# Attention over field pairs: rows fetched one by one from SyncE and ScalarE, the first lookup's numbers spread by TensorE

## The reference

```python
emb = jax.vmap(lambda tbl, idx: tbl[idx], in_axes=(0, 1), out_axes=1)(embed_tables, sparse)   # 2048 x 26 x 32
bi = emb[:, FIRST, :] * emb[:, SECOND, :]                                                     # 2048 x 325 x 32
a = jax.nn.relu(jnp.einsum('bpd,dh->bph', bi, att_w_w) + att_w_b)                             # 8 hidden units
scores = jnp.einsum('bph,ho->bpo', a, att_d_w) + att_d_b
att_weight = jax.nn.softmax(scores, axis=1)
att_out = jnp.sum(att_weight * bi, axis=1)
out = jax.nn.sigmoid(jnp.concatenate([att_out, dense], axis=-1) @ fin_w + fin_b)
```

## Time and profile before

| | before |
|---|---|
| runs | 483.49, 484.43, 484.66 us |
| profiled execution, its own time | 483.39 us |
| its span, first to last instruction | 481.6 us |
| TensorE busy | 450.2 us (93%), 2280 matmuls |
| VectorE busy | 372.6 us (77%) |
| GpSimd busy | 347.9 us (72%), 372 instructions |
| ScalarE busy | 95.8 us (20%) |
| mean granted TensorE clock | 0.996 of full speed |

### The profile page before, as it was taken

One profiled execution on the slowest core, in us unless ns is written; L12 is line 12 of the kernel. 1 busy time (PEld: TensorE's weight loads), 2 busy tenths in 40 slices (PEclk: granted clock), 3 DMA queues, 4 the chain that ended last, 5 costly groups with the idle time before them and its releaser, 6 DMA issues.

```text
span 481.6 us, 6198 instructions
## 1 busy us (share of the span) xinstructions
PE 450.2 (93%) x2280; PEld 177.6 (37%) x2280; DVE 372.6 (77%) x645; ACT 95.8 (20%) x198; POOL 347.9 (72%) x372
## 2 busy tenths in 40 slices
PE   0699999999998999999999899999999899999884
PEld 0354443343333533333333443333334344333221
DVE  6337788796965979799775969879786788887985
ACT  0000101131252011112243101113234201114253
POOL 5777777777777777777777777777777777777740
PEclk9999999999999999999999999999999999999998
DMA  6933743121122223222112222213111222322210
GB/s 221 250 13 15 147 58 36 13 15 13 15 13 15 14 14 79 15 14 14 14 14 13 15 13 15 13 13 15 14 13 16 14 15 13 15 13 14 15 10 1
DMA packets 13661, 15.06 MB, mean 31 GB/s; under 512 B 6368, under 2 KB 12608, under 8 KB 13248
## 3 DMA queue, kind: packets, MB, share of 16 engines
q0 software_dynamic: 11776, 6.05, 23.1%
q1 hardware_dynamic: 1360, 7.53, 4.2%
q10 hardware_dynamic: 496, 1.09, 0.6%
HBM read 14.61 MB, written 0.03 MB: 30 GB/s over the span
## 4 chain that ended last, share of the span: by engine, by line
PE 78%; POOL 8%; DVE 5%; issue 4%; DMA 3%; ACT 1%; POOLq 0%; DVEq 0%
PE looked_own L391 33%; PE back_s L391 16%; PE first L405 13%; PE sums_f L415 12%; POOL emb L368 8%; PE sums_s L429 3%; DVE onehot L667 2%; DMA chunk_numbers<-index_chunk 1%; DMA emb<-tables,rows 1%; DMA chunk_of<-chunk_numbers 1%; PE back_f L442 1%; PE back_s L452 1%; DVE look_masked L678 1%; DMA par<-params 1%; DVE ring L691 0%
## 5 line engine op out<-in xcount | busy, mean ns | idle before, releaser
L368 POOL DMA_INDIRECT emb<-tables,rows x324 | 305.9, 944 | 98.7 <-issue 96.9
L691 DVE TENSOR_TENSOR ring<-emb_t,turned 128x512 f32<-128x512 f32 (+9 forms) x180 | 193.9, 1114 | 3.4
L391 PE MATMUL looked_own<-look_table,onehot 128*128 128x448 f32 x434 | 178.0, 554 | 17.0 <-DVE onehot L667 16.7
L391 PEld LDWEIGHTS looked_own<-look_table,onehot 128*128 128x128 f32 x434 | 79.5, 192 | 114.4 <-issue 114.4
L507 ACT ACTIVATE hidden<-first,par 128x512 f32<-128x512 f32 (+1 forms) x84 | 56.5, 678 | 284.7 <-PE first L405 284.4
L391 PE MATMUL back_s<-look_table,onehot 128*128 128x448 f32 x238 | 94.4, 545 | 3.1 <-DVE score L739 3.1
L405 PE MATMUL first<-ring,par 128*32 128x512 f32 (+1 forms) x672 | 90.7, 591 | 4.3 <-DVE ring L691 4.3
L415 PE MATMUL sums_f<-ring,par 128*32 128x512 f32 (+1 forms) x672 | 90.0, 583 | 0.0
L667 DVE TENSOR_TENSOR onehot<-chunk_of,turned 128x2048 f32<-128x2048 f32 (+1 forms) x24 | 48.3, 2018 | 26.6 <-PE looked_own L391 21.2
L391 PEld LDWEIGHTS back_s<-look_table,onehot 128*128 128x128 f32 x238 | 44.0, 190 | 51.7 <-issue 51.7
L368 POOL DMA_INDIRECT emb<-tables,rows_first x44 | 41.8, 950 | 17.2 <-issue 13.1
(11 more groups left out here) (56 smaller groups left out, 101.0 us busy)
## 6 DMA issues: line engine op xcount, KB each, us to landing
emb<-tables,rows POOLq DMA_INDIRECT x324, 3.2
look_table<-tables SPq DMA_DIRECT2D x3, 1568.0 KB, 8.2
chunk_of<-chunk_numbers SPq DMA_DIRECT2D x3, 768.0 KB, 4.9
chunk_of<-chunk_numbers ACTq DMA_DIRECT2D x1, 768.0 KB, 3.8
emb<-tables,rows_first POOLq DMA_INDIRECT x44, 3.8
par<-params ACTq DMA_DIRECT2D x1, 258.5 KB, 3.1
ids<-sparse SPq DMA_DIRECT2D x1, 208.0 KB, 2.5
feats<-dense SPq DMA_DIRECT2D x1, 104.0 KB, 8.1
```

Source lines behind the costliest of these rows:

```text
L368: pool.indirect_dma_start(emb[:, f, g * D:(g + 1) * D], None, stacked, bass.IndirectOffsetOnAxis(ap=row, axis=0),).then_inc(gathered[f], 16)
L391: mm = nc.tensor.matmul(looked_rows[look_bank[tile]], onehot[:, c, g * P:(g + 1) * P], look_table[:, n, c, :], start=c == 0, stop=c == CHU ...
L691: nc.vector.tensor_tensor(slot[:, at:at + n, :], emb_t[:, i:i + n, :], turned[:, f % 2, :].unsqueeze(1).broadcast_to((P, n, P)), ALU.mult) ...
```

## The change

1. **SyncE fetches seven tiles of field 24.** For tile 3 of quad 0 and tiles 2 and 3 of the quads 1 to 3, SyncE loads 32 row numbers at a time into registers and issues one DMA of 128 bytes for each row: 7 x 128 = 896 DMAs into a new buffer `emb_placed`. Tile 2 of quad 0 is gathered into that buffer by GpSimd, ahead of its field 13. ScalarE copies the placed columns into `emb` ahead of the groups of field 23 (`place_rows`).
2. **ScalarE fetches four tiles of field 23** (tile 3 of each quad) in the same way: 8 rows ahead of the groups of each of the fields 0 to 15, 128 DMAs per quad, 512 in all (`fetch_rows`), with 16 row numbers loaded at a time.
3. **GpSimd** loses these 11 tiles' gathers plus the placed one, gets the placed one back early and one gather for field 19 in the last quad: 368 - 12 + 1 + 1 = 358.
4. **TensorE** looks up 11 tiles instead of 12 in the last quad. Its last two steps, which stood beside the fields 15 and 16, are gone.
5. **The first lookup's numbers** no longer go through HBM: TensorE multiplies one column of the identity, broadcast, with `index_chunk` (four matmuls into PSUM, `chunk_first`), and VectorE compares from there, ahead of the second `make_rows`. Table 0 is loaded in two parts, and the first steps wait for the first part alone.
6. **Queues.** Table 1 follows table 0 at once; table 2 and the second quad's chunk numbers come after SyncE's first 32 rows, the third quad's behind its first three tiles and the last quad's behind its fifth. The dense features move to ScalarE's queue. VectorE computes the row numbers for 1 and 2 in six small operations.

The core of the diff:

```diff
+ROWS_SP = 32
+SP_FIELD = 24
+TILES_SP = (1, 2, 2, 2)
+PLACED = 2
+SP_PLACE = 23
+SP_FIRST = 13
+LAST_LOOK_TILES = (4, 4, 3)
+ROW_FIELD = 23
+ROWS_LOADED = 16
+ROWS_BESIDE = 8
+ROWS_BESIDE_FIELDS = range(16)
@@ block.sync
-            sp.wait_ge(transposed, 6)
-            load_table(2)
-            for q in range(2, QUADS):
-                load_chunks(q)
+            sp.wait_ge(sp_rows_ready, 1)
+            tiles = 0
+            for q in range(QUADS):
+                for i in range(PLACED - TILES_SP[q], PLACED):
+                    t = q * G + G - PLACED + i
+                    for p in range(0, P, ROWS_SP):
+                        if tiles == 0 and p == P // 4:
+                            load_table(2)
+                            sp.wait_ge(chunk_numbers_home, 16)
+                            load_chunks(1)
+                        _, at = nc.values_load_multi_w_load_instructions(
+                            sp_rows[t:t + 1, p:p + ROWS_SP], engines=(mybir.EngineType.SP,), min_val=0,
...
+                        for k in range(ROWS_SP):
+                            sp.dma_start(emb_placed[p + k:p + k + 1, q, i * D:(i + 1) * D],
+                                         stacked[bass.ds(at[k], 1), :]).then_inc(sp_gathered[tiles], 16)
+                    tiles += 1
+                if 0 < q < QUADS - 1:
+                    load_chunks(q + 1)
@@ block.tensor
+            pe.wait_ge(index_chunk_made, 1)
+            for g in range(G):
+                row = ident[0:QUADS * LOOKS * G, g:g + 1].broadcast_to((QUADS * LOOKS * G, P))
+                mm = nc.tensor.matmul(chunk_first[:, g * P:(g + 1) * P], row, index_chunk[:], start=True, stop=True)
+            mm.then_inc(chunk_first_spread, 1)
...
-                    pe.wait_ge(look_table_in[n], 16)
+                    pe.wait_ge(look_table_first_in if n == 0 and part == 0 else look_table_in[n], 16)
@@ block.scalar
+                def place_rows():
+                    act.wait_ge(placed_gathered, (QUADS * PLACED - sum(TILES_SP)) * 16)
+                    for i in range(sum(TILES_SP[:q]), sum(TILES_SP[:q + 1])):
+                        act.wait_ge(sp_gathered[i], P * 16)
+                    nc.scalar.activation(emb[:, SP_FIELD, PLACED_COLS], emb_placed[:, q, :], ACT.Copy
+                                         ).then_inc(placed, 1)
+                def fetch_rows(f):
+                    at = ROWS_BESIDE_FIELDS.index(f) * ROWS_BESIDE
+                    if at == 0 and q == 0:
+                        act.wait_ge(row_numbers_ready, 1)
+                    if at == 0 and q:
+                        act.wait_ge(transposed, (q - 1) * F + ROW_FIELD + 1)
+                    if at % ROWS_LOADED == 0:
+                        _, numbers[:] = nc.values_load_multi_w_load_instructions(
...
+                    for p in range(at, at + ROWS_BESIDE):
+                        act.dma_start(emb[p:p + 1, ROW_FIELD, (G - 1) * D:], stacked[bass.ds(numbers[p % ROWS_LOADED], 1), :]
+                                      ).then_inc(rows_fetched, 16)
+                fetch_rows(0)
                 for f in range(1, F):
+                    if f in ROWS_BESIDE_FIELDS:
+                        fetch_rows(f)
+                    if f == SP_PLACE:
+                        place_rows()
                     done = groups_of(f)
```

More of the change, by code:

```diff
@@ L58, in attention_fm, with look_tiles @@
     LOOKS = len(LOOK)
+    assert max(LAST_LOOK_TILES) <= G and LAST_LOOK_TILES[0] == LOOK_TILES[0]
     assert P * PART_ROWS >= V and P * PART_ROWS - V <= V and LOOK[-1] < F - 1 and CHUNK_ROWS * D <= PAIRS_C * P
-    steps = [(q, n, g, part) for q in range(QUADS) for n in range(LOOKS) for g in range(G - LOOK_TILES[n], G)
+    def look_tiles(q, n):
+        return LOOK_TILES[n] if q < QUADS - 1 else LAST_LOOK_TILES[n]
+    steps = [(q, n, g, part) for q in range(QUADS) for n in range(LOOKS) for g in range(G - look_tiles(q, n), G)
              for part in range(len(STEPS))]
@@ L68, in attention_fm, with tiles_through_look @@
     assert len(STEP_FIELDS) + END_STEPS == STEPS_Q and END_STEPS == len(STEPS)
-    def tiles_through_look(n):
-        return sum(LOOK_TILES[:n + 1])
+    def tiles_through_look(q, n):
+        return q * TILES_Q + sum(look_tiles(q, i) for i in range(n + 1))
     def first_step(q, n):
-        return q * STEPS_Q + (tiles_through_look(n) - LOOK_TILES[n]) * len(STEPS)
+        return (tiles_through_look(q, n) - look_tiles(q, n)) * len(STEPS)
     def steps_beside(q, f):
@@ L86, in onehots_for @@
     def onehots_for(numbers):
-        return [(steps[i][0], steps[i][1], steps[i][3]) for i in numbers if steps[i][2] == G - LOOK_TILES[steps[i][1]]]
+        return [(steps[i][0], steps[i][1], steps[i][3]) for i in numbers if steps[i][2] == G - look_tiles(*steps[i][:2])]
     def tiles_ended(numbers):
@@ L113, in taken_before, with gathers_of @@
         return max([t + 1 for t in range(tile) if look_bank[t] == look_bank[tile]], default=0)
-    def gathers_of(f):
+    def gathers_of(q, f):
         if f in LOOK:
-            return G - LOOK_TILES[LOOK.index(f)]
-        return G
+            return G - look_tiles(q, LOOK.index(f))
+        if f == ROW_FIELD:
+            return G - 1
+        return G - PLACED if f == SP_FIELD else G
+    assert ROW_FIELD not in LOOK and ROWS_BESIDE * len(ROWS_BESIDE_FIELDS) == P and ROWS_LOADED % ROWS_BESIDE == 0
+    assert ROWS_BESIDE_FIELDS[-1] < ROW_FIELD
+    PLACED_COLS = slice((G - PLACED) * D, G * D)
+    assert FIRST_FIELDS <= SP_FIRST < SP_PLACE < SP_FIELD and len(TILES_SP) == QUADS and max(TILES_SP) <= PLACED
+    assert SP_FIELD not in LOOK
     assert G * D == P and B % (P * G) == 0 and RING < GROUPS and 1 < END_GROUPS
@@ L211, in attention_fm @@
             "p (t f) -> p t f", f=F) for i in range(2))
+        row_clamped, row_wrap = (final[0:QUADS].rearrange("p g e -> p (g e)")[:, i * P:(i + 1) * P] for i in range(2))
+        index_clamped, index_wrap, index_part = (
+            final[0:QUADS * LOOKS * G].rearrange("p g e -> p (g e)")[:, G * P + i * P:G * P + (i + 1) * P] for i in range(3))
+        sp_clamped, sp_wrap = (weighed[0:T].rearrange("p g e -> p (g e)")[:, i * P:(i + 1) * P] for i in range(2))
         neg_max = sb("neg_max", [P, G])
@@ L251, in attention_fm @@
         rows_ready = sem("rows_ready")
+        sp_ids_in = sem("sp_ids_in")
+        sp_steps = sem("sp_steps")
+        sp_rows_ready = sem("sp_rows_ready")
+        sp_gathered = [sem(f"sp_gathered{i}") for i in range(sum(TILES_SP))]
+        placed_gathered = sem("placed_gathered")
+        placed = sem("placed")
+        row_ids_in = sem("row_ids_in")
+        row_steps = sem("row_steps")
+        row_numbers_ready = sem("row_numbers_ready")
+        rows_fetched = sem("rows_fetched")
         gathered = [sem(f"gathered{f}") for f in range(F)]
@@ L360, in _ @@
                         pool.wait_ge(rows_ready, 1)
-                    if q and gathers_of(f):
+                    if q == 0 and f == SP_FIRST:
+                        for n in range(QUADS):
+                            for i in range(PLACED - TILES_SP[n]):
+                                t = n * G + G - PLACED + i
+                                pool.indirect_dma_start(
+                                    emb_placed[:, n, i * D:(i + 1) * D], None, stacked,
+                                    bass.IndirectOffsetOnAxis(ap=rows[:, t, SP_FIELD:SP_FIELD + 1], axis=0),
+                                ).then_inc(placed_gathered, 16)
+                    if q and gathers_of(q, f):
                         pool.wait_ge(transposed, (q - 1) * F + f + 1)
-                    for g in range(gathers_of(f)):
+                    for g in range(gathers_of(q, f)):
                         if q == 0 and f < FIRST_FIELDS:
@@ L606, in _, with make_onehots @@
                                     ).then_inc(index_chunk_made, 1)
+            dve.wait_ge(par_in, 16)
+            dve.wait_ge(sp_ids_in, 16)
+            nc.vector.tensor_scalar(sp_clamped[:], sp_ids[:], float(-V), float(V - 1), ALU.max, ALU.min
+                                    ).then_inc(sp_steps, 1)
+            dve.wait_ge(sp_steps, 1)
+            nc.vector.tensor_scalar(sp_wrap[:], sp_clamped[:], 0.0, float(V), ALU.is_lt, ALU.mult).then_inc(sp_steps, 1)
+            dve.wait_ge(sp_steps, 2)
+            nc.vector.scalar_tensor_tensor(sp_rows[:], sp_clamped[:], float(SP_FIELD * V), sp_wrap[:], ALU.add, ALU.add
+                                           ).then_inc(sp_rows_ready, 1)
+            def make_onehots(of, n, part):
+                tiles, chunks = slice((G - look_tiles(of, n)) * P, G * P), STEPS[part]
+                numbers, here = chunk_of[:, of % 2, n, tiles], chunk_here
+                if of == 0 and n == 0:
+                    dve.wait_ge(chunk_first_spread, 1)
+                    numbers, here = chunk_first[:, tiles], par[:, cols["look_chunk"]]
+                else:
+                    dve.wait_ge(chunk_of_in[of % 2], (of // 2 + 1) * 16)
```

(17 more changed lines are left out.)

66 lines of the change are left out of this document (39 added, 27 removed).

## The result

| | before | after |
|---|---|---|
| runs beside each other | 484.55 us (483.49 to 484.75, 4 runs) | 489.95 us (489.01 to 491.27, 4 runs) |
| profiled execution, its own time | 483.39 us | 491.27 us |
| span | 481.6 us | 489.4 us |
| TensorE busy | 450.2 us, 2280 matmuls | 453.6 us, 2274 matmuls |
| mean granted clock | 0.996 | 0.984 |

The changed kernel is slower: ratio 1.0117, 95% interval 1.0092 to 1.0142. The forecast was 475.6 us and faster; the time came out as rival A's. The profiled execution is the longest of the four after, and the shortest of the four before, so the spans differ by 7.8 us where the medians differ by 5.4.

The account below looks back on a forecast made before the run. TensorE paces three quads; TensorE, VectorE's pair products and GpSimd's queue meet at the end. Gain 11.8 (start 6.4, tile 3.6, gather waits 1.8) less 3.0 for late relus, 8.8 us: 475.6 us, range 470 to 493.

Parts of the forecast that it names:

- rival A: ScalarE's rows, dearer than forecast, pace TensorE in the quads; gain gone at 0.456 us a row, 483 to 500 us; chance 0.20.
- I take 0.42: Price in us of each single-row DMA on SyncE and ScalarE, taken between bounds of 0.33 and 0.60.
- part 4: Cost of the single rows on SyncE and ScalarE: SyncE's hidden, ScalarE's late relus costing TensorE 3.0 us in all.
- break-even at 0.456: Row price in us on ScalarE at which late relus eat the whole gain of 11.8 us.
- rival B: Loading row numbers counts, so a SyncE row takes 0.60 us and SyncE sets the end, about 570 us; chance 0.07.
- 0.407 us a row is free; every 0.01 us above costs 0.96 us a quad: ScalarE in quad 1: row price allowed by 96 DMAs and four relus of 0.69 us ahead of TensorE's first score products.
- also hidden: SyncE's queue: table 2 and later quads' chunk numbers issue in time behind the rows, the last near 275 us, needed near 315.
- SyncE's rows hidden: SyncE's 896 rows at 0.42 us end at 383 us, in time for field 24 of the last quad; 0.49 allowed.
- Part 1, the start: First lookup at 10.0 us instead of 16.36, a gain of 6.4 us that goes through to the end if gathers are in time.
- Parts 2 and 3: Gathers stay in time, GpSimd 10 gathers or 12.5 us ahead at the end; the last quad's missing tile gains VectorE 3.6 us.
- part 3: End of the kernel: VectorE's path gains 6.4 + 3.6 + 1.8 = 11.8 us, GpSimd's 12.5; the later one, 11.8, counts.
- Rival C: Many small transfers delay gathers by 4 us through shared DMA engines, losing 4 to 8 us, 480 to 484 us; chance 0.10.

Follow-up runs that it names:

- the kernel with spread rows: Changed kernel with ScalarE's 512 rows placed 6 ahead of each of fields 0 to 11 and 8 ahead of 12 to 18; 485.85 us, ratio 1.0046 to the kernel before.
- the 474.64 us kernel: Changed kernel with ScalarE's rows spread over 19 fields and the last quad's chunk numbers issued right behind the third quad's; 474.64 us, ratio 0.9804 to the kernel before.
- the start alone: Kernel before with only the spread chunk numbers, split table and earlier table and chunk-number loads; no single rows, 368 gathers, 12 tiles; 484.56 us, ratio 1.0002.

## Why the prediction was wrong

**The step that failed: "I take 0.42" in part 4.** The issue alone was sized right, 0.42 us on SyncE and 0.38 on ScalarE. The loading of the numbers was named as an unknown and then priced at nothing: with it (1.30 us for 16 numbers, 0.08 a row) and the longer first row behind each load a row takes 0.481. The prediction's own line, wrong if a row costs over 0.45 us on ScalarE, was crossed. Rival A was the right mechanism, with 0.20: its formula at 0.481 gives 484.4 - 11.8 + 96 x 2.5 x 0.074 = 490.4, and 489.95 was measured. That it comes so near is in part luck, as the next paragraphs show; and where the formula has half a quad's loss in the last quad, the relus cost TensorE more there, 8.2 us of waits, than in either of the two before. The middle of the bounds, 0.33 and 0.60, is 0.465, also on the losing side; choosing low between them, with the break-even at 0.456, was a choice of the sign.

The Trainium skill, page "Runtime: NRT & Kernel Launch", section "Instruction fetch mechanics", gives about 200 ns a register for loads from HBM; here a number loaded from SBUF costs 0.081 us on ScalarE, and 2.15 us for 32, 0.067, on SyncE. By the page SyncE's row would have been 0.62, as the prediction worked out, and rival B right; the measurement decides, 0.48, and it lies between the page and the prediction's zero.

**"0.407 us a row is free; every 0.01 us above costs 0.96 us a quad": near, by two errors that cancel.** A relu hardly holds the issuing, though it runs 0.69 us:

```profile
177.56 0.23 ACTq L644 DMA_DIRECT2D emb<-tables  x1
177.84 0.69 ACT L588 ACTIVATE hidden<-first,par 128x512 f32<-128x512 f32 x1 [26.97 <-issue]
177.98 0.23 ACTq L644 DMA_DIRECT2D emb<-tables  x1
```

From one row to the next are 0.42 us with the relu between them, and 0.39 without ((196.72 - 193.98) / 7). So only the relu that TensorE waits for counts with its 0.69, the three ahead of it with 0.03 each, and the free price is about (41.8 - 0.8) / 96 = 0.427. TensorE's waits for relus in quad 1 come to 1.95 + 0.75 + 2.07 = 4.8 us rather than 96 x 0.074 = 7.1. But the waits also cost clock, which the prediction did not have. Behind the third of them TensorE's granted clock stood at the lower of its two levels for 3.4 us, 0.50 of full speed; with both stalls gone there is no such stretch in quad 1:

```profile
197.20:200.60 3.40, 2.79 (x16) 0.61 (x16) 0.23 (x1) 0.55 (x1) 2.48 (x4) 0.50 0.31 43
```

That is most of the 2.0 us more of busy TensorE. Together 6.8.

**Chunk numbers "also hidden": wrong, and covered.** At 0.479 a row the last quad's go out at 318.65, not 275, and the kernel with spread rows wants them 8.7 us before they land. Priced by experiment it is 485.85 to 474.64, 11.2 us. In the changed kernel itself they cost nothing, because the relus are later still. The step that failed is the same: the prediction had these numbers needed near 315, and issued at 275 at 0.42 us a row.

**SyncE's rows hidden: right, with nearly nothing to spare.** The budget was 0.49 us a row. In the 474.64 us kernel the last row goes out at 443.94, (443.94 - 8.55) / 896 = 0.486, and no wait for `emb_placed` shows. VectorE waits three times for ScalarE's copy of the placed columns, 2.8 us in all and never over 0.9; these waits are in the 474.64 us kernel too.

**Part 1, the start: nearly.** TensorE's lookups start at 10.29 (forecast 10.0). The first 14 take 8.48 us instead of 7.71, so the gain at their end is 5.3 us, not 6.4. They begin at half pace: the matmuls of 448 columns start 0.75 us apart until 16.3 us and 0.375 apart from there, before until 20.9, which is 6.0 us at half pace against 4.5. (The profile's records of the granted clock begin only at 16.3 and 20.8, so its 1.00 for the windows ahead of them says nothing.) With the same start the 474.64 us kernel had 3.6 us at half pace and took 7.26 for the 14, so this differs from run to run; what sets it no run here shows. The prediction took one length for granted.

**Parts 2 and 3.** 358 gathers, the last at 451.86 (forecast 450.7): right. The step from field 17 to 18 is 2.93 us (forecast 2.9): right, though the tile is worth 2.8 us in the end rather than 3.6, since VectorE then waits for gathers. Start and tile together: 484.2 - 474.6 = 9.6 us with the two stalls gone, where part 3 summed 11.8. So the gain that the prediction argued is there, less a fifth, and ScalarE's and SyncE's queues take all of it and more.

**Rival C** is not seen, with the DMA engines 24 to 31% busy before rather than the prediction's 20 to 25: the median gather lands in 3.6 us instead of 3.2, and in 2.6 in the 474.64 us kernel; no field of the first three quads waits for one. Nor are the rows spread over many DMA engines. Packets of SyncE's queue in the start alone, then in the changed kernel:

```profile
q1 hardware_dynamic: 1400, 7.43, 4.1%
q1 hardware_dynamic: 3192, 7.55, 4.3%
```

1792 packets more for 896 rows are two for each row. On which engine they ran the profile does not show.

**Ledger.** Before 484.2; start alone 0; start, rows and tile with both stalls removed -9.6; the stalls of the relus and the chunk numbers, lying over one another, +15.3; after 489.95. The kernels were timed on different chips, where the kernel before took 483.6 to 484.6 us, so each term is good to about 1 us.

## What to carry to other kernels

A DMA whose address comes from a register costs its issue and the load of that register: count both, on the engine that issues, and hold the sum against the break-even before anything else. When work is put into an in-order queue, list everything behind it with the time at which it is needed, and look for a second late item under the first, since removing one of two stacked stalls shows little. Put rare, long-known transfers ahead of long series of small ones.

## What the runs showed of the hardware

- A 128-byte row fetched by its own DMA: 0.38 us of issue on ScalarE and 0.42 on SyncE, 0.48 on both with its number loaded; the two queues side by side cost each other nothing (27.01 and 26.91 us for 56 rows of ScalarE, 168.42 and 168.65 for 352 of SyncE). Each row was two DMA packets.
- A relu of 0.69 us between two of ScalarE's rows made their distance 0.42 us instead of 0.39.
- Behind three waits of TensorE of 1.95, 0.75 and 2.07 us its granted clock was 0.50 for 3.4 us (197.2 to 200.6), and 0.94 over 178 to 200; without these waits it was 1.00 there. The same matmuls kept it busy 453.6 us in all, against 447.6 without the stalls.
- The first lookups ran at half pace for 3.6 to 6.0 us, and the same 14 matmuls took 7.26 to 8.50 us from run to run.
- On one chip the same kernel took 731 us instead of 484, and there kernels with more instructions lost up to 10.5%.
